# A graph layer's message lists: step columns made by ScalarE, and one product that takes differences

## The chip, the cores and the metric

One core of one Trainium2 chip runs the whole program. The metric is the device time of one execution in microseconds (us), lower is better. The chip has a matrix engine (TensorE, PE), a vector engine (VectorE, DVE), a scalar engine (ScalarE, ACT), a general engine (GpSimd, POOL) and a queue that mostly issues transfers (SyncE, SP). "PEld" is PE's loading of the stationary operand, which overlaps its products.

## The reference

Two layers. The first, a relational graph layer, is the one the change is in; the second is a mixture of experts (16 experts, 2 per token) and takes the second half of the time.

```python
x = x + gnn(layernorm(x), src, dst, edge_type)      # x is [625, 512]
x = x + moe(layernorm(x))

def gnn(input, heads, tails, rel, ...):              # 10625 edges, 8 relations
    h_self = input @ W_self.T + b_self
    H_all = einsum('rod,nd->rno', W_rel, input) + b_rel[:, None, :]   # 16 relations (8 each way)
    msg_to_heads = H_all[rel, tails]
    msg_to_tails = H_all[rel + R, heads]
    agg = segment_sum(msg_to_heads, heads) + segment_sum(msg_to_tails, tails)
    return relu(h_self + agg)
```

## The kernel before

**The products.** H_all has 16 relations by 5 tiles of 125 nodes, so 80 products, numbered i = 0 to 79 (`product`, L819). j = i // 5 is the relation, t = i % 5 the tile. Each is 12 matmuls of 512 columns, since every float32 operand is split into a high and a low part (hi\*hi, hi\*lo, lo\*hi over four chunks). ACT copies each finished product out of PSUM (`take`, L678, its copy is L682), then puts the bias of the product after next into the PSUM buffer that became free (`bias_in`, L691); PE waits for that before product i + 2. SP stores the tile in DRAM (`h_dram`). The weights of relation j + 1 are split while relation j runs: ACT makes the high part of one chunk (`w_main`, L676), DVE the low part (`w_rest`, L503), one chunk in each iteration with t of 1 to 4.

**The lists.** A message is a row of H_all added to a node. The kernel sorts messages into blocks of 128 lanes that belong to one node tile: 90 blocks for direction d = 0, 100 for d = 1. From each edge the number of its block (`block_at`) and its lane in it (`lane`) have been computed in a [125 x 85] layout (`places`, L512). The list, that is which edge stands in which lane of which block, is built by matmul: for each of the 85 edge columns c, DVE writes a one-hot matrix `lane_hot` [125 edges x 128 lanes] (L529) and a matrix `told_hot` [125 edges x blocks, twice] which holds the edge's node and relation at its block (L531 for d = 0, L536 twice for d = 1). PE multiplies the two and adds up over the 85 columns in the PSUM bank `p_list` (`list_chunk`, L848, L855), five columns at a time. Three sets of five columns rotate. `read_list` (L541) then turns `p_list` into the row numbers of the gathers (`row_of`) and the target node of each lane (`seg_of`).

**The messages.** For each block POOL issues an indirect gather of 128 rows from `h_dram` (L400), up to ten blocks ahead. ACT makes their high part (L697), DVE a one-hot matrix of the targets (L555) and the low part (L559), and PE adds both into `p_sum` (L864, L865).

**The order of work is written out by hand.** One loop over i stands in each engine's program, and everything is put into it by tables:

- `columns(d, i)` (L287) says how many of the 85 columns are made before iteration i: `min(85, int(each * (i - begin)))`, with (begin, each) of (4, 5.5) for d = 0 and (24, 3) for d = 1. It gives 5 or 6 columns in each of iterations 4 to 18 and the last three (82 to 84) in iteration 19; for d = 1 it gives 3 in each of iterations 24 to 51 and the last one (84) in iteration 52.
- `chunks(d, i)` (L296): PE multiplies a chunk of five behind product i if its columns were made before iteration i. The last chunk is an exception: it stands behind product 19 for d = 0 and behind product 52 for d = 1, so in the iteration that makes its last columns.
- `due(i)` (L283): three messages per iteration, which PE takes in i = 23 to 37 and from 43 on. ACT and DVE prepare them one iteration earlier.
- `read_list(0)` stands in DVE's iteration 20, behind `told_of(1)`; `read_list(1)` in its iteration 53. `places(1)` stands in DVE's iteration 21, behind that iteration's `w_rest`.

The engines' orders inside an iteration are:

```text
ACT:  w_main, take(i), bias_in(i + 2), [carry_in in i = 8..12], messages
DVE:  w_rest, [told_of(1) in 20, places(1) in 21], columns, read_list, messages
PE:   product(i), list chunks, messages
POOL: waits for rows_ready and the stores, then gathers
```

The function `product` waits for `h_biased`, `message` on PE for `part_lo`, and the first gather for `rows_ready`, which the last instruction of `read_list` (L549) raises. After the 80th product the remaining messages, the self product, a second layernorm and the experts follow in order.

Of the kernel before, what the change touches and what calls it, by code (L numbers as in the profile page):

```python
# [22 lines left out]
P = 128  # L23
# [44 lines left out]
def build(nc, x, edges, w_self, b_self, w_rel, b_rel, router_w, gate_w, up_w, down_w, out):  # L68
    ctx = ExitStack()
    with ctx:  # L70
# [62 lines left out]
        bias_rows_loaded = [sem(f"bias_rows_loaded{i}") for i in range(BIAS_ROWS)]  # L133
        h_stored = [sem(f"h_stored{i}") for i in range(OUTS)]
        list_hot, list_taken, rows_ready = sem("list_hot"), sem("list_taken"), sem("rows_ready")
        part_hi, part_lo, block_done = sem("part_hi"), sem("part_lo"), sem("block_done")
        var2_ready, root2_ready, ln2_ready = sem("var2_ready"), sem("root2_ready"), sem("ln2_ready")
        scale2_ready, xn_hi_ready = sem("scale2_ready"), sem("xn_hi_ready")
# [1 line left out]
        gathers_issued = sem("gathers_issued")  # L140
        x2_full, x2_copied, logits_full = sem("x2_full"), sem("x2_copied"), sem("logits_full")
        round_sems = range(steps.num, logits_full.num + 1)
        assert len(round_sems) == 54 + OUTS + BIAS_ROWS


        ln2_stored, gap_ready, exp_ready = sem("ln2_stored"), sem("gap_ready"), sem("exp_ready")
# [28 lines left out]
        with ExitStack() as g:  # L175
# [5 lines left out]
            x2_whole = sb("x2_whole", [P, T, D], F32, g)  # L181
            x2 = x2_whole[0:TP]
            bias_rows = [x2_whole[:, k] for k in range(BIAS_ROWS)]

            carry = sb("carry", [TP, T, D], F32, g)
            trip = sb("trip", [P, 1], F32, g)
# [100 lines left out]
            def columns(d, i):  # L287

                begin, each = LISTS[d]
                return max(0, min(EC, int(each * (i - begin))))  # L290

            def chunked(d, i):

                return columns(d, i if columns(d, i) == EC else i - 1) // HOT
# [67 lines left out]
            def on_gpsimd(pool, nth_round):  # L362
                q = nc.gpsimd
                done = 0

                def then(instruction):
                    nonlocal done
                    done += 1
                    instruction.then_inc(pool_steps, 1)
                    pool.wait_ge(pool_steps, done)  # L370

                for n, (d, low, _, c) in enumerate(SPANS):
                    if low == 0:
                        q.memset(held[:, d], float(c * P))
                        i = q.memset(first_block[:, d], 0.0)
                i.then_inc(edge_consts, 1)
                q.memset(zero_rows, 0.0).then_inc(route_consts, 1)
                for n, (_, _, _, c) in enumerate(SPANS):
                    q.memset(per_block[:, 0, n * T:(n + 1) * T], 1 / (c * P))
                    i = q.memset(per_block[:, 1, n * T:(n + 1) * T], (c * P + 1) / 2 / (c * P))  # L380
                i.then_inc(edge_consts, 1)
                q.tensor_copy(block_iota[:], iota_i[0:EP, 1:1 + max(IN_DIR)])
                q.tensor_copy(seg_iota[:], iota_i[:, 1:1 + TP])
                q.tensor_copy(slot_iota[:], iota_i[0:TP, 0:P]).then_inc(edge_consts, 1)
                q.iota(token_id_i[:], [[TP, T]], base=1, channel_multiplier=1)
                then(q.iota(spare_row_i[:], [[0, 1]], base=N + 1, channel_multiplier=1))
                q.tensor_copy(token_id[:], token_id_i[:])
                q.tensor_copy(spare_row[:], spare_row_i[:])
                q.tensor_copy(expert_iota[:], iota_i[0:TP, 0:NX])
                q.tensor_copy(tile_iota[:], iota_i[0:1, 0:LISTED])  # L390
                pool.wait_ge(spare_cleared, 64)
                for b in range(BLOCKS):
                    if b in span_at:
                        n = span_at[b]
                        pool.wait_ge(rows_ready, SPANS[n][0] + 1)
                        for k in range(OUTS):
                            pool.wait_ge(h_stored[k], 32 * len(range(k, made(n), OUTS)))
                    if b >= ROWS:
                        pool.wait_ge(part_lo if b - ROWS < last_span else block_done, b - ROWS + 1)
                    q.indirect_dma_start(rows_sb[:, b % ROWS], None, h_dram[0:1 + made(n) * TP],  # L400
                                         bass.IndirectOffsetOnAxis(ap=row_of[:, b:b + 1].bitcast(U32), axis=0)
                                         ).then_inc(gathered[b % ROWS], 16)
                q.tensor_scalar(trip[:], trip[:], 1.0, None, ALU.add).then_inc(gathers_issued, 1)
                pool.wait_ge(gathers_issued, 1)
                pool.wait_ge(round_counted, 1)
                pool.reg_load(rounds_of(pool), n_rounds[0:1, 0:1])

            def on_vector(dve, nth_round):
# [103 lines left out]
                def places(d):  # L512

                    place, here, nth = place_in[:, d], temp[:, 0, d], temp[:, 1, d]
                    then(v.scalar_tensor_tensor(place, place, BIG, held_before[:, d], ALU.subtract, ALU.subtract))
                    v.tensor_tensor(here, place, held[:, d], ALU.is_lt)
                    then(v.tensor_scalar(nth, place, (P - 1) / 2, 1 / P, ALU.subtract, ALU.mult))
                    then(v.tensor_scalar(nth, nth, ROUND, None, ALU.add))
                    v.tensor_scalar(nth, nth, ROUND, None, ALU.subtract)
                    then(v.scalar_tensor_tensor(here, place, 0.0, here, ALU.is_ge, ALU.mult))  # L520
                    v.scalar_tensor_tensor(lane[:, d], nth, -float(P), place, ALU.mult, ALU.add)
                    then(v.scalar_tensor_tensor(nth, nth, 1.0, first_block[:, d], ALU.add, ALU.add))
                    then(v.tensor_tensor(block_at[:, d], nth, here, ALU.mult))

                def column(d, c):
                    n, k, wide = (EC // HOT) * d + c // HOT, c % HOT, IN_DIR[d]
                    if k == 0 and n >= HOT_SETS:
                        dve.wait_ge(list_taken, n - HOT_SETS + 1)
                    v.tensor_scalar(lane_hot[:, n % HOT_SETS, k], slot_iota[:], lane[:, d, c:c + 1], None, ALU.is_equal)  # L529
                    if d == 0:  # L530
                        i = v.scalar_tensor_tensor(told_hot[:, n % HOT_SETS, k, 0:2 * wide].rearrange("p (a b) -> p a b", a=2),  # L531
                                                   block_iota[:, 0:wide].unsqueeze(1).to_broadcast([EP, 2, wide]), block_at[:, d, c:c + 1],
                                                   told0[:, :, c:c + 1].to_broadcast([EP, 2, wide]), ALU.is_equal, ALU.mult)
                    else:
                        for what in range(2):
                            i = v.tensor_scalar(told_hot[:, n % HOT_SETS, k, what * wide:(what + 1) * wide], block_iota[:, 0:wide],  # L536
                                                block_at[:, d, c:c + 1], told1[:, what, c:c + 1], ALU.is_equal, ALU.mult)
                    if k == HOT - 1:
                        i.then_inc(list_hot, 1)

                def read_list(d):  # L541
                    wide, at = IN_DIR[d], IN_DIR[0] * d
                    node, rel_seg, rel = p_list[:, 0:wide], p_list[:, wide:2 * wide], rel_of[:, 0:wide]
                    dve.wait_ge(list_taken, (EC // HOT) * (d + 1))
                    then(v.tensor_scalar(rel, rel_seg, (P - 1) / 2, 1 / P, ALU.subtract, ALU.mult))
                    then(v.tensor_scalar(rel, rel, ROUND, None, ALU.add))
                    then(v.tensor_scalar(rel, rel, ROUND, None, ALU.subtract))
# [67 lines left out]
                for i in range(PRODUCTS):  # L615
# [17 lines left out]
                    for d in range(2):  # L633
                        for c in range(columns(d, i), columns(d, i + 1)):
                            column(d, c)
                        if columns(d, i - 1) < EC and columns(d, i) == EC:
                            read_list(d)
                            if d == 0:
                                round_count()
# [18 lines left out]
            def on_scalar(act, nth_round):  # L658
# [27 lines left out]
                def bias_in(i):  # L686
# [2 lines left out]
                        act.wait_ge(bias_rows_loaded[j % BIAS_ROWS], 16 * (j // BIAS_ROWS + 1))  # L689
                    act.wait_ge(h_taken, i - 1)  # L690
                    s.copy(p_h[0:TP, i % 2], bias_rows[j % BIAS_ROWS][0:TP]).then_inc(h_biased, 1)  # L691

                def message(b):
                    act.wait_ge(gathered[b % ROWS], nth_round * (16 * BLOCKS // ROWS) + 16 * (b // ROWS + 1))
# [55 lines left out]
                for i in range(2, PRODUCTS):  # L750
# [5 lines left out]
                    take(i)  # L756
                    if 8 <= i < 8 + T:
                        carry_in(i - 8)
                    for b in range(due(i), due(i + 1)):
                        message(b)  # L760
                act.wait_ge(gate_loaded, 32)
# [22 lines left out]
            def on_tensor(pe, nth_round):  # L784
# [63 lines left out]
                def list_chunk(d, n):  # L848
                    nth, wide = (EC // HOT) * d + n, 2 * IN_DIR[d]
                    pe.wait_ge(list_hot, nth + 1)  # L850
                    if d and n == 0:
                        pe.wait_ge(rows_ready, d)
                    for k in range(HOT):
                        c = n * HOT + k
                        i = m.matmul(p_list[:, 0:wide], lane_hot[:, nth % HOT_SETS, k], told_hot[:, nth % HOT_SETS, k, 0:wide],  # L855
                                     start=(c == 0), stop=(c == EC - 1))
                    i.then_inc(list_taken, 1)

                def message(b):
                    o = p_sum[0:TP, tile_of[b]]  # L860
# [48 lines left out]
                for i in range(PRODUCTS):  # L909
# [12 lines left out]
                    for d in range(2):  # L922
                        for n in chunks(d, i):
                            list_chunk(d, n)
                    for b in range(due(i - 1), due(i)):
                        message(b)
                left = range(due(PRODUCTS - 1), last_span)
# [810 lines left out]
```

## Time and profile before

| | |
|---|---|
| median of 3 runs | 737.27 us (736.48 to 740.19) |
| the profiled execution | 733.35 us, of which the span of instructions is 731.6 us |
| PE busy | 694.9 us (95%) |
| DVE busy | 625.8 us (86%) |
| ACT busy | 502.0 us (69%) |
| POOL busy | 309.9 us (42%) |
| mean granted TensorE clock | 0.985 of full speed |

Times inside the trace count from the start of the span. A busy time is the union of an engine's instruction spans. What ended an idle time is inferred from semaphore events. The 80 products run from 15 to 348 us, the experts from about 400 us to the end.

### The profile page before, as it was taken

Reading aid. Unit: us, or ns where it says so; the run is one execution under the profiler, and the core shown is the slowest. Engines: PE = TensorE matmul, PEld = TensorE weight load, DVE = VectorE, ACT = ScalarE, POOL = GpSimd, SP = SyncE. Lnnn points to the kernel's source line nnn. Section 1 sums busy time; section 2 is a strip of 40 time slices with the busy share of each in tenths; the row PEclk is TensorE's granted clock in tenths of the full one; section 3 lists DMA queues with packets and bytes.
Section 4 is the critical chain, followed back from the end, with each engine's and each line's share of the span. In section 5 each row is a group of like instructions: output and inputs, shape, how many; then the busy total and the mean of one; then the engine's idle time right before and its main releaser. Section 6 shows DMA issues by size and latency. Waiting matters only on the chain. (4 is left out here: it accounts for less than half of the span.)

```text
span 731.6 us, 10688 instructions
## 1 busy us (share of the span) xinstructions
PE 694.9 (95%) x3210; PEld 542.9 (74%) x3210; DVE 625.8 (86%) x1289; ACT 502.0 (69%) x717; POOL 309.9 (42%) x279
## 2 busy tenths in 40 slices
PE   5899999999998999999997999999999999999993
PEld 4777766777676777777755788888888888888883
DVE  8889979998999677777775899999998999999990
ACT  3655476665675777777556498888877888888870
POOL 3000077851787677777771033332234333333201
PEclk9999999999999999999998899999999999999997
DMA  7347589884888889998767989999999999999932
GB/s 243 126 144 270 168 267 305 299 257 144 301 281 295 276 280 306 315 295 244 217 196 239 379 321 354 405 394 392 405 355 396 370 379 374 361 403 379 357 110 30
DMA packets 54436, 212.75 MB, mean 291 GB/s; under 512 B 9753, under 2 KB 10150, under 8 KB 39158
## 3 DMA queue, kind: packets, MB, share of 16 engines
q1 hardware_dynamic: 34998, 153.85, 55.9%
q0 software_dynamic: 19392, 58.35, 27.4%
q8 instruction: 21, 0.34, 0.2%
q14 instruction: 25, 0.20, 0.1%
HBM read 184.36 MB, written 27.80 MB: 290 GB/s over the span
## 5 line engine op out<-in xcount | busy, mean ns | idle before, releaser
L400 POOL DMA_INDIRECT rows_sb<-h_dram,row_of x190 | 212.5, 1119 | 165.3 <-DVE row_of L549 84.1
L559 DVE TENSOR_TENSOR rows_lo<-rows_sb,rows_hi 128x512 fp32r<-128x512 f32 x175 | 120.1, 686 | 43.5 <-ACT rows_hi L697 43.4
L830 PE MATMUL p_h<-g_hi_sb,xt_hi_whole 128*125 128x512 f32 x320 | 128.4, 401 | 0.3 <-DVE g_lo_sb L503 0.3
L831 PE MATMUL p_h<-g_lo_sb,xt_hi_whole 128*125 128x512 f32 x320 | 126.7, 396 | 0.0
L832 PE MATMUL p_h<-g_hi_sb,xt_lo_whole 128*125 128x512 f32 x320 | 126.5, 395 | 0.0
L697 ACT CAST rows_hi<-rows_sb 128x512 fp32r<-128x512 f32 x175 | 100.1, 619 | 25.5 <-DMA rows_sb<-h_dram,row_of 23.3
L682 ACT COPY h_whole<-p_h 125x512 f32<-125x512 f32 x80 | 46.9, 586 | 89.2 <-PE p_h L832 89.1
L1195 POOL DMA_INDIRECT tokens<-token_dram,rows_of_tokens x15 | 22.1, 1470 | 170.8 <-ACT rows_of_tokens L1484 131.5
L864 PE MATMUL p_sum<-rows_hi,seg_hot 128*125 128x512 f32 x175 | 73.6, 421 | 5.4 <-DVE rows_lo L559 4.5
L1248 DVE TENSOR_TENSOR u_lo_sb<-stage_up,u_hi_sb 128x2048 fp32r<-128x2048 f32 x34 | 76.4, 2288 | 1.0
L1248 DVE TENSOR_TENSOR d_lo_sb<-stage_down,d_hi_sb 128x2048 fp32r<-128x2048 f32 x32 | 71.8, 2286 | 3.0 <-ACT d_hi_sb L1469 2.9
L1599 PE MATMUL p_gate<-g_hi_sb,xt_lo_whole 128*128 128x512 f32 x256 | 74.1, 401 | 0.0
L1248 DVE TENSOR_TENSOR g_lo_sb<-stage_gate,g_hi_sb 128x2048 fp32r<-128x2048 f32 x32 | 71.9, 2287 | 1.1 <-ACT g_hi_sb L1469 1.1
L1599 PE MATMUL p_up<-u_hi_sb,xt_lo_whole 128*128 128x512 f32 x256 | 72.7, 395 | 0.0
L832 PEld LDWEIGHTS p_h<-g_hi_sb,xt_lo_whole 128*125 128x125 f32 x320 | 59.6, 186 | 15.1
L830 PEld LDWEIGHTS p_h<-g_hi_sb,xt_hi_whole 128*125 128x125 f32 x320 | 59.8, 187 | 14.6 <-issue 0.3
L831 PEld LDWEIGHTS p_h<-g_lo_sb,xt_hi_whole 128*125 128x125 f32 x320 | 59.8, 187 | 14.1
L865 PE MATMUL p_sum<-rows_lo,seg_hot 128*125 128x512 f32 x175 | 69.1, 395 | 0.0
L1469 ACT CAST u_hi_sb<-stage_up 128x2048 fp32r<-128x2048 f32 x34 | 63.3, 1914 | 4.1 <-PEq L1011 4.1
L1469 ACT CAST g_hi_sb<-stage_gate 128x2048 fp32r<-128x2048 f32 x32 | 59.6, 1915 | 6.5 <-PE p_gate L1599 6.5
L1469 ACT CAST d_hi_sb<-stage_down 128x2048 fp32r<-128x2048 f32 x32 | 59.6, 1916 | 0.0
L1206 POOL DMA_INDIRECT out<-y_sb,rows_of_out x16 | 30.4, 1899 | 66.5 <-ACT y_sb L1509 66.2
(292 smaller groups left out, 1363.6 us busy)
## 6 DMA issues: line engine op xcount, KB each, us to landing
stage_up<-in_L_ffn_up_w SPq DMA_DIRECT2D x34, 1024.0 KB, 8.0
stage_gate<-in_L_ffn_gate_w SPq DMA_DIRECT2D x32, 1024.0 KB, 8.7
stage_down<-in_L_ffn_down_w SPq DMA_DIRECT2D x32, 1024.0 KB, 7.5
h_dram<-h_whole SPq DMA_DIRECT2D x80, 224.0 KB
stage_up<-in_L_gnn_W_rel SPq DMA_DIRECT2D x16, 1024.0 KB, 8.0
x_whole<-in_L_gnn_b_rel SPq DMA_DIRECT2D x16, 256.0 KB, 9.7
rows_sb<-h_dram,row_of POOLq DMA_INDIRECT x190, 5.1
h_dram<-h_whole SPq DMA_DIRECT2D x80, 26.0 KB
```

The lines of the kernel that those rows point to most:

```text
L400: q.indirect_dma_start(rows_sb[:, b % ROWS], None, h_dram[0:1 + made(n) * TP], bass.IndirectOffsetOnAxis(ap=row_of[:, b:b + 1].bitcast(U32 ...
L559: v.tensor_tensor(rows_lo[:, b % PARTS], rows_sb[:, b % ROWS], rows_hi[:, b % PARTS].bitcast(F32), ALU.subtract).then_inc(part_lo, 1)
L682: s.copy(h_sb[:, i % OUTS], p_h[0:TP, i % 2]).then_inc(h_taken, 1)
L697: s.copy(rows_hi[:, b % PARTS], rows_sb[:, b % ROWS]).then_inc(part_hi, 1)
L830: m.matmul(o, xt_hi[:, dc, at], wt_hi_sb[:, 1 - j % 2, dc], start=(by_matmul and dc == 0), stop=False, skip_group_check=True)
L831: m.matmul(o, xt_hi[:, dc, at], wt_lo_sb[:, 1 - j % 2, dc], start=False, stop=False, skip_group_check=True)
L832: last = m.matmul(o, xt_lo[:, dc, at], wt_hi_sb[:, 1 - j % 2, dc], start=False, stop=False, skip_group_check=True)
L864: m.matmul(o, seg_hot[:, b % HOTS], rows_hi[:, b % PARTS], start=False, stop=False, skip_group_check=True)
L865: m.matmul(o, seg_hot[:, b % HOTS], rows_lo[:, b % PARTS], start=False, stop=False, skip_group_check=True).then_inc(block_done, 1)
L1248: v.tensor_tensor(half(w_lo[k][:], k, i), staged(k, e, i), half(w_hi[k][:], k, i).bitcast(F32), ALU.subtract).then_inc(split_lo[k], 1)
L1469: s.copy(half(w_hi[k][:], k, i), staged(k, e, i)).then_inc(split_hi[k], 1)
L1599: i = m.matmul(into[:, h * 512:(h + 1) * 512], x_part[of_first(e)][:, c], w_part[k][:, c, h * 512:(h + 1) * 512], start=(c == 0 and x_part ...
```

## The change

The lane matrix is no longer a one-hot matrix. ACT writes, for each column, the sign of (m + 0.5 - lane) over the lanes m = 0 to 127: -1 below the edge's lane and +1 from it on. PE adds these up as before, so that `p_list` holds running sums over the lanes. DVE halves them into SBUF (`halve`), and one float32 product with a [128 x 128] matrix of differences (`difference`) writes the list into `p_list`. DVE no longer makes lane columns. POOL makes the constants at the start. `list_end(d)` is the first iteration in which all columns have been made: 20 and 53.

```diff
+            differ, shifted, corner = [x2_whole[:, 3, k * P:(k + 1) * P] for k in range(3)]
+            between = x2_whole[0:TP, 3, 3 * P:4 * P].bitcast(F16)[:, 0:P]
+            sums = x2_whole[:, 4, 0:2 * max(IN_DIR)]
...
+            def list_end(d):
+                return min(i for i in range(PRODUCTS) if columns(d, i) == EC)
...  on POOL, behind tile_iota and ahead of the wait for spare_cleared
+                q.tensor_scalar(between, iota_i[0:TP, 0:P], 0.5, None, ALU.add).then_inc(steps_made, 1)
+                q.affine_select(out=shifted, in_=ones[:], compare_op=ALU.is_equal, fill=0.0, base=1, pattern=[[-1, P]], channel_multiplier=1)
+                then(q.affine_select(out=corner, in_=ones[:], compare_op=ALU.is_equal, fill=0.0, base=1 - P, pattern=[[-1, P]],
+                                     channel_multiplier=1))
+                then(q.tensor_tensor(differ, ident[:], shifted, ALU.subtract))
+                q.tensor_tensor(differ, differ, corner, ALU.add).then_inc(steps_made, 1)
...  on DVE, in places(d), column(d, c), and read_list(d)
-                    v.scalar_tensor_tensor(lane[:, d], nth, -float(P), place, ALU.mult, ALU.add)
+                    v.scalar_tensor_tensor(lane[:, d], nth, float(P), place, ALU.mult, ALU.subtract).then_inc(placed, 1)
...
-                    v.tensor_scalar(lane_hot[:, n % HOT_SETS, k], slot_iota[:], lane[:, d, c:c + 1], None, ALU.is_equal)
...
+                def halve(d):
+                    dve.wait_ge(list_taken, (EC // HOT) * (d + 1))
+                    if d:
+                        dve.wait_ge(differed, d)
+                    v.tensor_scalar(sums[:, 0:2 * IN_DIR[d]], p_list[:, 0:2 * IN_DIR[d]], 0.5, None, ALU.mult).then_inc(halved, 1)
...
-                    dve.wait_ge(list_taken, (EC // HOT) * (d + 1))
+                    dve.wait_ge(differed, d + 1)
...  DVE's loop
-                        if columns(d, i - 1) < EC and columns(d, i) == EC:
+                        if i == list_end(d):
+                            halve(d)
+                        if i == list_end(d) + 1:
                             read_list(d)
                             if d == 0:
                                 round_count()
...  on ACT
+                def lane_step(d, c):
+                    n, k = (EC // HOT) * d + c // HOT, c % HOT
+                    if c == 0:
+                        act.wait_ge(placed, d + 1)
+                        if d == 0:
+                            act.wait_ge(steps_made, 1)
+                    if k == 0 and n >= HOT_SETS:
+                        act.wait_ge(list_taken, n - HOT_SETS + 1)
+                    i = s.activation(lane_hot[:, n % HOT_SETS, k], between, ACT.Sign, bias=lane[:, d, c:c + 1], scale=1.0)
+                    if k == HOT - 1:
+                        i.then_inc(lane_steps, 1)
...  ACT's loop, behind take(i) and carry_in, ahead of the messages
+                    for d in range(2):
+                        for c in range(columns(d, i), columns(d, i + 1)):
+                            lane_step(d, c)
...  on PE
                     pe.wait_ge(list_hot, nth + 1)
+                    pe.wait_ge(lane_steps, nth + 1)
...
+                def difference(d):
+                    if d == 0:
+                        pe.wait_ge(steps_made, 2)
+                    pe.wait_ge(halved, d + 1)
+                    m.matmul(p_list[:, 0:2 * IN_DIR[d]], differ, sums[:, 0:2 * IN_DIR[d]], start=True, stop=True).then_inc(differed, 1)
...  PE's loop, behind the chunks and ahead of the messages
+                        if i == list_end(d):
+                            difference(d)
```

## Rows read from the trace of the kernel before

**Rows 1.** Busy time by stretch: us, then PE, PEld, DVE, ACT, POOL; clock; DMA
```profile
118.00:165.00 47.00, 46.77 (x211) 34.16 (x210) 47.00 (x161) 32.80 (x60) 33.06 (x27) 1.00 0.85 278
190.00:228.00 38.00, 37.85 (x171) 27.85 (x172) 38.00 (x130) 26.78 (x49) 30.38 (x26) 1.00 0.87 287
```

**Rows 2.** Timeline (start, us): ACT takes products 18, 19, 21, 22, 30, 35
```profile
83.96 0.59 ACT L682 COPY h_whole<-p_h 125x512 f32<-125x512 f32 x1 [1.47 <-PE p_h L832]
...
87.17 0.59 ACT L682 COPY h_whole<-p_h 125x512 f32<-125x512 f32 x1 [1.39 <-PE p_h L832]
...
94.18 0.59 ACT L682 COPY h_whole<-p_h 125x512 f32<-125x512 f32 x1 [1.01 <-PE p_h L832]
...
96.97 0.59 ACT L682 COPY h_whole<-p_h 125x512 f32<-125x512 f32 x1 [1.03 <-PE p_h L832]
...
135.29 0.59 ACT L682 COPY h_whole<-p_h 125x512 f32<-125x512 f32 x1 [1.96 <-PE p_h L832]
...
158.59 0.59 ACT L682 COPY h_whole<-p_h 125x512 f32<-125x512 f32 x1 [1.96 <-PE p_h L832]
```

**Rows 3.** Timeline: a column of the second list on DVE
```profile
132.21 0.25 DVE L529 TENSOR_SCALAR lane_whole<-slot_iota,lane 125x128 f16<-125x128 f16 x1
...
132.37 0.75 DVE L536 TENSOR_SCALAR told_whole<-block_iota,block_at,told 125x100 f16<-125x100 f16 x2
```

**Rows 4.** Groups of instructions by form, ACT: busy us, mean ns, idle before
```profile
L676 ACT CAST g_hi_sb<-stage_up 128x512 fp32r<-128x512 f32 x64 | 38.9, 618 | 0.0
...
L674 ACT ACTIVATE g_hi_sb<-stage_up,first 128x512 fp32r<-128x512 f32 x4 | 2.9, 722 | 0.0
...
L725 ACT ACT_TABLE_LOAD x1 | 1.3, 1283 | 4.7 <-PEq L949 4.7
```

**Rows 5.** Timeline: three copies of 512 columns in a row on ACT
```profile
103.52 1.67 ACT L697 CAST rows_hi<-rows_sb 128x512 fp32r<-128x512 f32 x3
```

**Rows 6.** ACT's idle time ahead of the takes: 43 to 70 us
```profile
  PE p_h L832: 10.7, 8
```

**Rows 7.** Timeline: the take of product 13, PE's chunks behind product 14
```profile
67.48 0.59 ACT L682 COPY h_whole<-p_h 125x512 f32<-125x512 f32 x1 [0.92 <-PE p_h L832]
...
70.48 0.95 PE L855 MATMUL p_list<-told_whole,lane_whole 125*128 125x180 f16 x10
```

**Rows 8.** ACT's idle time ahead of the takes: 76 to 89 us
```profile
  PE p_h L832: 5.8, 4
```

**Rows 9.** Timeline: PE's last chunk of the first list
```profile
88.00 0.56 PE L855 MATMUL p_list<-told_whole,lane_whole 125*128 125x180 f16 x5 [0.46 <-DVE told_whole L531]
```

**Rows 10.** Timeline: reading the first list, the first gather, the first messages
```profile
90.45 0.25 DVE L545 TENSOR_SCALAR rel_of<-p_list 128x90 f32<-128x90 f32 x1
...
91.38 0.24 DVE L549 SCALAR_TENSOR_TENSOR row_of<-rel_of,p_list 128x90 int32<-128x90 f32 x1
...
92.52 1.19 POOL L400 DMA_INDIRECT rows_sb<-h_dram,row_of  x1 [84.14 <-DVE row_of L549]
...
93.20 0.70 DVE L503 TENSOR_TENSOR g_lo_sb<-stage_up,g_hi_sb 128x512 fp32r<-128x512 f32 x1 [0.36 <-ACT g_hi_sb L676]
...
95.59 0.25 DVE L523 TENSOR_TENSOR block_at<-temp 125x85 f32<-125x85 f32 x1
...
102.68 0.51 PE L864 MATMUL p_sum<-rows_hi,seg_hot 128*125 128x512 f32 x1 [1.64 <-DVE rows_lo L559]
```

**Rows 11.** Timeline: seven float32 matmuls of 512 columns in a row
```profile
378.92 3.17 PE L871 MATMUL p_sum<-rows_sb,told_whole 128*125 128x512 f32 x7
```

**Rows 12.** Timeline: the take of product 52, the second list's last chunk
```profile
231.00 0.59 ACT L682 COPY h_whole<-p_h 125x512 f32<-125x512 f32 x1 [0.80 <-PE p_h L832]
...
233.20 0.60 PE L855 MATMUL p_list<-told_whole,lane_whole 125*128 125x200 f16 x5 [2.24 <-DVE told_whole L536]
```

**Rows 13.** Timeline: two later waits of PE for messages, products 26 and 43
```profile
117.41 0.49 PE L864 MATMUL p_sum<-rows_hi,seg_hot 128*125 128x512 f32 x1 [1.23 <-DVE rows_lo L559]
...
189.91 0.49 PE L864 MATMUL p_sum<-rows_hi,seg_hot 128*125 128x512 f32 x1 [0.89 <-DVE rows_lo L559]
```

More of the change, by code:

```diff
@@ L135, in build @@
         list_hot, list_taken, rows_ready = sem("list_hot"), sem("list_taken"), sem("rows_ready")
+        steps_made, placed, lane_steps, halved, differed = sem("steps_made"), sem("placed"), sem("lane_steps"), sem("halved"), sem("differed")
         part_hi, part_lo, block_done = sem("part_hi"), sem("part_lo"), sem("block_done")
@@ L142, in build @@
         round_sems = range(steps.num, logits_full.num + 1)
-        assert len(round_sems) == 54 + OUTS + BIAS_ROWS
+        assert len(round_sems) == 59 + OUTS + BIAS_ROWS
         ln2_stored, gap_ready, exp_ready = sem("ln2_stored"), sem("gap_ready"), sem("exp_ready")
```

## Prediction

> **What bounds the kernel now.** I read the busy time by stretch first. While the second list is made and messages flow, PE is busy nearly throughout, but DVE is busy for the whole of both stretches, ACT for 70% [rows 1]. Two engines can't both be the bound, so I asked the timeline how long a product lasts. ACT takes each product when it ends, so the takes are a clock. A product alone lasts 2.79 us (96.97 - 94.18), thus a matmul 0.2325; with one chunk of the first list it is 3.21 (87.17 - 83.96), so a chunk costs 0.42; with three messages, six matmuls more, it should be 4.18. From product 30 to 35 there are three chunks: 5 x 4.18 + 3 x 0.42 = 22.2. Measured is 23.3 [rows 2]. So DVE does set the pace there, by 0.22 us a product, in small waits that a busy share hides. In the first list DVE does not: PE's steps there are those of its own work.
>
> The messages start tightly: PE waits for the third one, at 102.68, and this goes back to the first gathers, which POOL issued at 92.52 as soon as the list was read [rows 10]. What the change does to that moment matters as much as what it takes from DVE.
>
> **The change part by part.**
>
> *DVE loses the lane columns.* One has a span of 0.25, but the next instruction starts 0.16 behind it [rows 3]: 0.16 is what it costs in a row. Three per iteration give 0.48, more than the 0.22 by which DVE holds PE back. So PE becomes the bound. Some 20 products (27 to 37, 44 to 52) were paced by DVE: 20 x 0.22 = -4.4 us. Of the large wait ahead of the second list's last chunk (2.24, [rows 12]) a part goes: ACT makes column 84 behind the take of product 52 at 231.00, so at 231.00 + 0.62 + 0.53 + 0.40 + 0.05 = 232.6 instead of 233.2: -0.6.
>
> *The price of a step on ACT.* No row shows a Sign over 128 columns. A copy of 512 columns takes 0.62 and one that reads a scale from SBUF 0.72, so a pointer costs 0.10 [rows 4]. Three copies in a row take 1.67, so each overlaps the next by 0.10 [rows 5]. With some 0.82 ns a column (estimated: an instruction of 512 columns less a fixed part near 0.2), 128 columns take 0.62 - 0.32 + 0.10 = 0.40 alone and 0.30 in a row. Bounds are 0.20 (the pointer free) and 0.40 (no overlap). I take 0.30. The Trainium skill (ScalarE: Activation LUTs, What ACT_TABLE_LOAD costs) gives 280 ns + 0.833 N with a pointer bias and 93 ns of overlap, 0.294 in a row; by it the sum below would be 0.4 less. The same page (Rules for kernel authors) tells authors to do plain arithmetic on VectorE rather than on ScalarE. It speaks against this move, and the rows agree: 0.16 there, 0.30 here.
>
> *First list, ACT falls behind: +2.2.* Ahead of the takes of products 6 to 13 ACT idled 10.7 us in all [rows 6]; iterations 5 to 12 get 44 steps, 13.2 us. So the take of product 13 comes 2.5 late, at 69.95. Its six steps end at 69.95 + 1.15 (two copies, take and bias: 0.62 + 0.53) + 6 x 0.30 + 0.1 = 73.0. PE wants all of them for the second chunk behind product 14, which it began near 70.85 [rows 7]: +2.15. With steps of 0.24 or less it is nothing (44 x 0.24 is 10.7); with 0.40 it is about 6.
>
> *The last chunk of the first list: +2.1.* From there to product 19 ACT gets 22 steps more, 6.6 us against 5.8 idle [rows 8], and is 0.8 late again. Columns 82 to 84 are made behind take 19, since ACT's order ties them to it, while DVE made them while PE was still in product 19. So 87.17 + 0.8 + 1.15 + 0.9 + 0.1 = 90.1, against 88.0 [rows 9].
>
> *The differences: +0.8.* A float32 matmul of 512 columns takes 0.43 in a row [rows 11]. One of 180 or 200 columns with its load I put at 0.4, between 0.2 and 0.6; two of them. DVE halves (0.25) while PE is in the product ahead, so this hides.
>
> *The list is read an iteration later: +5.4.* This is the largest term and no instruction of it is new. Before, `read_list(0)` ran in DVE's iteration 20, from 90.45 to 91.62. Now it stands in iteration 21, and there behind two things. `w_rest` waits for ACT's `w_main`, which stands behind take 20: it ran from 93.20 to 93.90. Then `places(1)` ran to 95.84 [rows 10]. So `read_list` can end at 95.84 + 1.2 = 97.0 on the old clock, 5.4 later. The first gather moves from 92.52 to 97.9. Message 2 was already waited for, so what was late by 0 is now late by 5.4, and PE stands for it. POOL issues the later ones at its own pace, so they don't catch up. Bounds: 4 (landings are quicker away from the weight transfers) and 6. The second list's delay costs nothing: its gathers also need product 54 in DRAM, stored after take 54, and that ends later than DVE's `read_list(1)`.
>
> *POOL's five constants* run at the start, where POOL then waits 84 us for the list [rows 10]: nothing, or some tenths if they disturb DVE. ACT's steps among the messages (0.9 per iteration) fit its idle time in rows 1 (30% of a product, 1.4 us). If that cover is gone, messages come late: a rival below.
>
> **Sum:** 2.2 + 2.1 + 0.8 + 5.4 - 4.4 - 0.6 = +5.5 us. The experts start that much later, nothing there changes. The profiled execution took 733.35, the median of the runs is 737.27; on the median: 742.8. A measurement of this kernel can tell about 0.5% (3.7 us) from no change; the forecast is +0.75%.
>
> **The rivals.**
>
> 1. *ACT hides its steps and the messages make it up; not slower.* At 0.24 a step or less, the first list costs 0, its last chunk 1.1, the differences 0.8, the late reading 5.4. Against it 4.4 + 0.6, and PE's later waits for messages (1.23 and 0.89, [rows 13]) end too, as a DVE with time in hand prepares them earlier: +0.2, so 737.5. It decides at 0.24 us a step. For it: ACT idled before every take. Against: 0.30 from rows 4 and 5, and the wait at 117.41 looks like one for a gather, which a late start doesn't help. Chance 0.22. If the gathers landed faster too, it would reach faster by over 0.5%; I leave that 0.07 on top.
>
> 2. *The gathers or ACT bound the message stretch.* With steps of 0.3, ACT's iteration is 1.15 + 0.9 + 1.67 + 0.53 = 4.25 against PE's 4.18 to 4.6, and a late start leaves less lead for gathers. Then the 4.4 doesn't come: +9.9, 747.2. For it: little margin. Against: the sum per product still stays below PE's with a chunk. Chance 0.12.
>
> 3. *Sign needs tables of its own.* A table load takes 1.28 [rows 4]; one ahead of the first step would find ACT idle or add to its lag, a second ahead of the square roots after the messages would lie on the path: +6.8 to +8, about 744. Chance 0.05. The Trainium skill (ScalarE: Activation LUTs, Table sets) says that cheap functions such as relu, copy, identity and abs stand in every set; it doesn't name Sign there, and no run here shows it.
>
> **How the numbers follow.** My forecast has 0.54, and 0.44 of that is above +3.7. Slower: 0.44 + 0.12 + 0.05 = 0.61, less a hundredth for the measurement. Same: 0.10 of the forecast and rival 1's 0.22, 0.32. Faster: 0.07 and that hundredth, 0.08. The range takes in rival 1 at its lower end and rival 2 at its upper: 737 to 748.
>
> **What would show it.** Right: the lane rows on ACT start 0.30 apart in a row; ACT has no idle time ahead of takes 9 to 13; PE waits about 2 us for an ACT lane row behind product 14 and again behind product 19; L549's instruction ends more than 5 us later against the end of product 20, and PE's first message waits 4 to 6 us for `rows_lo`; five products in the message stretch take 22.2 rather than 23.3; no ACT_TABLE_LOAD more. Wrong: steps of 0.24 or less with no waits behind product 14; a first gather that is not late against product 20; message iterations still at 4.78, or gathers named as what ends ACT's waits in them.

## The result, and the profile after

The changed kernel takes 740.22 us (median of 20 runs, 737.31 to 747.01), the kernel before 737.95 (20 runs beside them). The ratio is 1.0044, 95% interval 1.0024 to 1.0065: slower by 3.2 us, 1.8 to 4.8. The medians alone differ by 2.3. The forecast was 742.8 with a range of 737 to 748. Its +5.5 us has the right sign but lies above that interval. Two executions, one of e1 below (746.71) and one of the kernel before beside e9 to e11 (745.35), lay over 1.5% above their fastest and are left out of the ratios.

The profiled executions differ by more: 740.55 against 733.35. The profiled execution of the kernel before was faster than each of its 20 timed runs (the lowest is 734.91). So the trace tells where time goes, and the ratios how much.

Busy time of each engine in the page after (us, share of the span, instructions):

```profile
PE 697.9 (94%) x3214; PEld 547.2 (74%) x3214; DVE 601.1 (81%) x1121; ACT 549.4 (74%) x887; POOL 309.9 (42%) x284
```

DVE lost 25 us of work and ACT gained 47; PE has 3 us more. The waits of PE (who waited for whom, total us, times, longest):

```profile
PE p_sum L909 <- DVE rows_lo L579: 7.7, 8, 3.0
PE p_list L893 <- ACT lane_whole L723: 4.7, 3, 2.1
```

In the first, the longest had been 1.64 [rows 10]; the second is new: two of its three stand where PE had waited for DVE, 0.46 and 2.24 [rows 9, 12], one behind product 14. The stretch of the first list and the first messages, in order of time (start, us, what, the idle time before it):

```profile
71.76 0.47 PE L893 MATMUL p_list<-told_whole,lane_whole 125*128 125x180 f16 x4 [0.89 <-ACT lane_whole L723]
...
88.26 0.57 ACT L704 COPY h_whole<-p_h 125x512 f32<-125x512 f32 x1
...
90.52 0.55 PE L893 MATMUL p_list<-told_whole,lane_whole 125*128 125x180 f16 x5 [2.12 <-ACT lane_whole L723]
...
97.26 0.69 DVE L518 TENSOR_TENSOR g_lo_sb<-stage_up,g_hi_sb 128x512 fp32r<-128x512 f32 x1 [4.39 <-ACT g_hi_sb L698]
...
99.62 0.25 DVE L538 TENSOR_TENSOR block_at<-temp 125x85 f32<-125x85 f32 x1
...
100.83 0.24 DVE L569 SCALAR_TENSOR_TENSOR row_of<-rel_of,p_list 128x90 int32<-128x90 f32 x1
...
107.11 0.50 PE L909 MATMUL p_sum<-rows_hi,seg_hot 128*125 128x512 f32 x1 [3.02 <-DVE rows_lo L579]
108.71 0.79 PE L909 MATMUL p_sum<-rows_hi,seg_hot 128*125 128x512 f32 x1 [0.87 <-DVE rows_lo L579]
```

These answer to [rows 7, 9, 10]. DVE stands idle for 4.39 us for ACT's `w_main`, then splits the weight, places the second list, and only then reads the first, as forecast: the list is complete near 95.6 and read at 101.1. The first gather goes out at 101.97, 6.5 us after the take of product 20 (95.47); before it was 1.1 us after it (92.52 and 91.41). That is the 5.4 of the forecast to the tenth. What it cost is another matter (below).

The steps: three in a row take 0.98 us, one alone 0.40, so the next starts 0.29 behind. ACT has no idle time at all ahead of the takes of products 6 to 13, where it had 10.7 us [rows 6].

```profile
116.91 0.98 ACT L723 ACTIVATE lane_whole<-x_whole,lane 125x128 f16<-125x128 f16 x3
...
144.22 0.59 ACT L704 COPY h_whole<-p_h 125x512 f32<-125x512 f32 x1 [0.97 <-PE p_h L869]
...
166.62 0.59 ACT L704 COPY h_whole<-p_h 125x512 f32<-125x512 f32 x1 [1.01 <-PE p_h L869]
```

The last two rows are the takes of products 30 and 35: 22.4 us for the five, where [rows 2] had 23.3. PE now sets the pace there, and ACT still idles about 1 us ahead of a take.

Something that no term of the forecast had: the granted TensorE clock. Busy time by stretch (us, then PE, PEld, DVE, ACT, POOL; the third figure from the end is the granted clock), and PE's matmuls inside the second stretch:

```profile
91.00:95.00 4.00, 4.00 (x12) 3.12 (x12) 1.74 (x10) 0.00 (x0) 0.00 (x0) 0.57 0.85 304
108.00:115.00 7.00, 6.29 (x14) 4.53 (x15) 5.99 (x15) 4.43 (x8) 5.48 (x6) 0.51 0.74 220
115.00:122.00 7.00, 7.00 (x30) 5.34 (x30) 4.44 (x16) 5.68 (x14) 5.48 (x6) 1.00 0.84 250
```

```profile
111.31 0.63 PE L868 MATMUL p_h<-g_lo_sb,xt_hi_whole 128*125 128x512 f32 x1
111.74 0.63 PE L869 MATMUL p_h<-g_hi_sb,xt_lo_whole 128*125 128x512 f32 x1
```

Behind PE's wait of 2.12 us, and again behind those of 3.02 and 0.87, the clock is at 1.2 GHz, and matmuls start 0.43 apart instead of 0.23. In the profiled execution of the kernel before, the clock was full throughout this stretch, with waits of at most 1.64 there. But it was full, too, behind the same wait of 2.12 in the profiles of e1 and e7 below. This is e1's row for the first of these stretches:

```profile
91.00:95.00 4.00, 4.00 (x20) 3.26 (x20) 2.42 (x14) 1.06 (x2) 0.00 (x0) 1.00 0.81 293
```

In e5, e9 and e12 it was low there again. So this half clock is not a fixed part of the change: it comes in some executions of that wait and not in others.

### The profile page after: what moved, and what is told of

Read it like the earlier page. It is cut to its first block and busy times, and to the rows that moved or that the text cites. A ratio compares the mean times of both kernels' runs of the same rounds, so it can differ in the third digit from the quotient of the medians.

```text
span 738.8 us, 10740 instructions
## 1 busy us (share of the span) xinstructions
PE 697.9 (94%) x3214; PEld 547.2 (74%) x3214; DVE 601.1 (81%) x1121; ACT 549.4 (74%) x887; POOL 309.9 (42%) x284
## 5 line engine op out<-in xcount | busy, mean ns | idle before, releaser
L867 PE MATMUL p_h<-g_hi_sb,xt_hi_whole 128*125 128x512 f32 x320 | 130.1, 406 | 1.1 <-ACT p_h L713 0.8
L868 PE MATMUL p_h<-g_lo_sb,xt_hi_whole 128*125 128x512 f32 x320 | 128.3, 401 | 0.0
L518 DVE TENSOR_TENSOR g_lo_sb<-stage_up,g_hi_sb 128x512 fp32r<-128x512 f32 x64 | 43.4, 686 | 28.8 <-ACT g_hi_sb L698 28.8
```

The source lines that it names most:

```text
L867: m.matmul(o, xt_hi[:, dc, at], wt_hi_sb[:, 1 - j % 2, dc], start=(by_matmul and dc == 0), stop=False, skip_group_check=True)
L868: m.matmul(o, xt_hi[:, dc, at], wt_lo_sb[:, 1 - j % 2, dc], start=False, stop=False, skip_group_check=True)
```

## The experiments

Theory: three independent terms, late reading of the first list (slower), ACT's load in the first list (slower), relief of DVE in the second (faster). Rivals: ACT's load explains all of the loss; the clock is a term of its own; the gathers set the time whatever is mended. Each kernel below was timed against the kernel before in the same series; a ratio of 1.001 is 0.74 us. Where two rows are compared, their difference is known to 2.5 to 4 us either way. Differences in us below are from the ratios.

| kernel | median us | ratio to before, 95% |
|---|---|---|
| the changed kernel | 740.22 | 1.0044 (1.0024 to 1.0065) |
| e1 changed, list read in iteration 20 | 736.58 | 0.9992 (0.9965 to 1.0019) |
| e2 before, list read in iteration 21 | 741.25 | 1.0050 (1.0025 to 1.0074) |
| e3 changed, last steps ahead of the take | 740.88 | 1.0054 (1.0022 to 1.0087) |
| e4 only the second list by steps | 731.79 | 0.9927 (0.9895 to 0.9958) |
| e5 changed, matmuls that bridge the wait | 743.25 | 1.0073 (1.0043 to 1.0103) |
| e6 e1 and e3 together | 737.35 | 1.0003 (0.9976 to 1.0031) |
| e7 only the first list by steps | 743.66 | 1.0096 (1.0056 to 1.0135) |
| e8 e4, last column made first | 731.82 | 0.9935 (0.9904 to 0.9966) |
| e9 changed, messages begun two products later | 735.77 | 0.9975 (0.9945 to 1.0005) |
| e11 before, messages begun two products later | 731.14 | 0.9921 (0.9889 to 0.9953) |
| e10 e8, messages begun two products later | 728.44 | 0.9878 (0.9836 to 0.9920) |
| e12 e1, messages begun two products later | 732.06 | 0.9907 (0.9872 to 0.9943) |

**e1, the list read in iteration 20**

```diff
-                        if i == list_end(d) + 1:
+                        if i == list_end(d) + d:
                             read_list(d)
```

> The changed kernel with the first list read in DVE's iteration 20 again, right behind its halving, ahead of that iteration's successor's w_rest and places. Theory 'late reading' (the move of read_list by one iteration is the largest cost): the first gather comes some 4.6 us earlier against product 20 than in the changed kernel, PE's wait for the first messages (3.0 + 0.9 us) shrinks to under 2, and with it the half clock behind it; total 4 to 7 us less than the changed kernel, so 0 to 3 us less than the kernel before. Rival 'ScalarE's load' (ACT's steps cost it all): the first gather moves but the messages stay late because ACT is; less than 1.5 us gained on the changed kernel.

Measured: 0.9992, so 3.8 us less than the changed kernel's 1.0044. The first gather goes out at 96.28 instead of 101.97, and PE's one wait for the first messages is 1.35 us (102.68 had 1.64 in [rows 10]). A little under the expected 4 to 7 and above the rival's 1.5, though with 2.5 us either way it doesn't exclude the rival by itself. A later wait for messages is longer, 1.80 at 120.01 against 1.23 in [rows 13].

**e2, the late reading alone, in the kernel before**

```diff
-                        if columns(d, i - 1) < EC and columns(d, i) == EC:
+                        k = i if d else i - 1
+                        if columns(d, k - 1) < EC and columns(d, k) == EC:
                             read_list(d)
```

> The kernel before with nothing changed but that the first list is read in DVE's iteration 21, behind w_rest and places, as in the changed kernel. Late reading: slower than before by 4 to 7 us (5.4 of waiting for the first messages, with or without some half clock behind it), that is about 742 to 745. ScalarE's load: within 1.5 us of before.

Measured: 1.0050, +3.7 us (1.8 to 5.5), a little under the expected 4 to 7, with no step on ACT at all. Its timeline, first gather and first messages:

```profile
96.54 0.24 DVE L549 SCALAR_TENSOR_TENSOR row_of<-rel_of,p_list 128x90 int32<-128x90 f32 x1
97.67 1.19 POOL L400 DMA_INDIRECT rows_sb<-h_dram,row_of  x1 [89.28 <-DMA h_dram<-h_whole]
...
101.22 0.62 ACT L698 CAST rows_hi<-rows_sb 128x512 fp32r<-128x512 f32 x1 [3.28 <-DMA rows_sb<-h_dram,row_of]
...
102.62 0.49 PE L865 MATMUL p_sum<-rows_hi,seg_hot 128*125 128x512 f32 x1 [3.15 <-DVE rows_lo L559]
...
104.09 0.79 PE L865 MATMUL p_sum<-rows_hi,seg_hot 128*125 128x512 f32 x1 [0.74 <-DVE rows_lo L559]
```

The first gather is where the forecast had put it (97.9). But ACT has its rows 3.55 us after the issue. The third gather, the one that PE had waited for, landed 6.0 us after its issue before and 3.6 here. So PE's first message is 3.1 us later than before (102.62 and 99.54), and its third 2.8, not 5.4. Behind the wait the clock falls, and product 24 is taken at 111.44, 5.2 later than before. Two products on, PE waits 0.35 where it waited 1.23 [rows 13], and the lateness is 4.1 and stays so (product 42 is taken at 188.89, before at 184.88). Moving one call by an iteration is about half of the whole loss; ACT's load is out as its only cause.

**e4, only the second list by steps.** The first list's lane columns stay on DVE, without halving and difference, read in iteration 20.

```diff
+                    if d == 0:
+                        v.tensor_scalar(lane_hot[:, n % HOT_SETS, k], slot_iota[:], lane[:, d, c:c + 1], None, ALU.is_equal)
...
-                    for d in range(2):
+                    for d in range(1, 2):
                         for c in range(columns(d, i), columns(d, i + 1)):
                             lane_step(d, c)
```

> Only the second list's lane columns are made by ACT as steps and differenced; the first list is made and read as before. My sum for this part alone: products 27 to 37 and 44 to 51 at the pace of PE, -0.12 to -0.22 us each (-2.4 to -4.4), -0.6 ahead of the last chunk, +0.4 for one difference: 2.5 to 4.5 us less than before. Rival 'gathers or ACT bound the message stretch': no gain, within 1 us of before or slower.

Measured: 0.9927, 5.4 us less (3.1 to 7.7), more than the expected 2.5 to 4.5, and faster than both kernels. So ACT and the gathers don't take the gain away. Gathers still cost something: its profiled execution is one of its two slowest (735.24, the median is 731.79), and in it PE waits 0.99 at 140.94 for messages. The same windows as [rows 1]:

```profile
118.00:165.00 47.00, 45.95 (x215) 35.35 (x213) 43.15 (x131) 41.06 (x91) 30.64 (x28) 1.00 0.88 292
190.00:228.00 38.00, 37.94 (x178) 29.46 (x177) 35.99 (x110) 34.28 (x75) 29.46 (x29) 1.00 0.91 300
```

In the same time PE does 215 and 178 matmuls instead of 211 and 171, DVE is no longer full, ACT has gone from 33 to 41 us of 47.

**e7, only the first list by steps**, the other half, read in iteration 21 as in the change (the mirror image of e4's edit).

> The other half of the change: only the first list by ACT's steps and a difference, read in DVE's iteration 21; the second list made and read as before. If the change is the sum of its halves, this half costs what the second-list half gained plus what the whole costs: 5.4 + 3 = some 8 us more than before (745 to 747). My own sum for it: about 1.1 behind product 14, 2.1 to 2.5 ahead of the last chunk, 0.4, and 3.7 to 5.4 of late reading: 7.3 to 9.4. Rival 'the halves share a cost' (clock or gathers): under 6.

Measured: 1.0096, +7.1 us (4.1 to 10), just under the 7.3 to 9.4 of my own sum. The halves add up to +1.7, the whole is +3.2; their intervals take that in. Of the 7.1, late reading is 3.7 (e2), so ACT's load in the first list is some 3.4; from e1 less e4 it is 4.8.

**e3, ACT's last steps ahead of the take**

```diff
+                    for d in range(2):
+                        if i == list_end(d) - 1:
+                            for c in range(columns(d, i), columns(d, i + 1)):
+                                lane_step(d, c)
                     take(i)
...
-                        for c in range(columns(d, i), columns(d, i + 1)):
-                            lane_step(d, c)
+                        if i != list_end(d) - 1:
+                            for c in range(columns(d, i), columns(d, i + 1)):
+                                lane_step(d, c)
```

> The changed kernel with ACT's last steps of each list (columns 82 to 84, and 84) ahead of the takes of products 19 and 52 instead of behind them. Tie to the take: PE's waits of 2.1 and 1.7 us ahead of the last chunks fall, the first to under 0.7, the second to what DVE's told column leaves (1.7 before in the second-list kernel, so 0 to 0.3 saved); the half clock behind product 19 goes with the first (1.5 us): 2 to 4 us less than the changed kernel. Rival: the first gathers depend on w_main and the takes, not on the chunk, and the saving is eaten by the wait for the first messages: under 1 us.

Measured: 1.0054, nothing gained that 2.8 us either way could show. The wait only changes its name and keeps 1.69 of its 2.12:

```profile
90.09 0.56 PE L898 MATMUL p_list<-told_whole,lane_whole 125*128 125x180 f16 x5 [1.69 <-DVE told_whole L545]
```

DVE's columns 82 to 84 stand behind its `w_rest`, and that behind ACT's `w_main`, which is late because of the steps before it. The take was not the only tie. In its profile product 20 is taken 2.0 us earlier, but 1.6 of that is the half clock, which is gone in e1 too, where the wait is unchanged. Against e1's 93.91 the edit gives 0.4 (93.51). The waits for the first messages (2.97, 0.81, 0.82) take 0.7 of the lead back. The rest doesn't vanish there: it is 2.3 us at product 42 and 1.4 at product 79, but the two profiled executions end alike (740.71 and 740.55), so this is within what executions differ by.

**e6, e1 and e3 together**

> Both mends at once: first list read in iteration 20, last steps ahead of the takes. If the terms add: 2 to 4 us less than the kernel with only the reading mended (736.6), that is 733 to 735, at the level of the second-list kernel or up to 2 us above (lag behind product 14 and one difference remain). Rival: gathers behind the weight transfer at product 25 set the time, and everything earlier is given back there: 736 to 737.

Measured: 1.0003 against 0.9992 for e1: nothing gained again; 737.35 is above both ranges, nearest the rival's. Its profile has product 20 at 93.53, 0.4 ahead of e1, as in e3: that is all that moving ACT's steps gives.

**e8, in e4 the last column made first on both engines**, ahead of the take and of `w_rest`.

> The second-list kernel (731.8) with its last column (84) made ahead of the take of product 52 on ACT and ahead of w_rest on DVE. PE's wait of 1.7 us ahead of the last chunk falls below 0.3: 1 to 1.6 us less, 730 to 731. If a later wait (gathers near product 61) takes it up: no difference.

Measured: 0.9935 against 0.9927, no difference, where 1 to 1.6 us less was expected. In the profile product 53 is taken 5.8 us after product 52 instead of 6.5, so 0.7 of the 1.7 went, too little to tell.

**e5, 16 matmuls of 512 columns behind product 23**, their result not used. They are extra work in PE's order and keep it at work while the first gathers land.

```diff
+                    if i == 23:
+                        pe.wait_ge(rows_ready, 1)
+                        for _ in range(16):
+                            m.matmul(p_list[0:TP, :], xt_hi[:, 0, 0:TP], xt_lo_whole[:, 0:512], start=True, stop=True)
```

> The changed kernel with 16 extra matmuls of 512 columns on PE behind product 23 (their result is not used), ahead of the wait for the first messages. They take 3.7 us at full clock inside a wait of over 3.9 us. Theory 'clock' (the halving behind that wait costs time of its own): TensorE stays at full clock behind the wait, product 24 lasts 2.8 us instead of 4.7, total 1.5 to 3 us less than the changed kernel. If the half clock is hidden by the gathers that are late anyway: within 1 us of the changed kernel.

Measured: 1.0073, 2.1 us more than the changed kernel, known to 2.7 either way. So the expected 1.5 to 3 us less is excluded, and whether it is really slower is not shown. The clock did stay full behind this wait: product 24 came 3.89 us after product 23, where the changed kernel needed 6.25. But PE then waited for the next gathers:

```profile
123.72 0.50 PE L909 MATMUL p_sum<-rows_hi,seg_hot 128*125 128x512 f32 x1 [1.06 <-DVE rows_lo L579]
126.30 0.50 PE L909 MATMUL p_sum<-rows_hi,seg_hot 128*125 128x512 f32 x1 [1.85 <-DVE rows_lo L579]
```

At product 25 it is 2.1 us ahead of the changed kernel, at product 27 it is 1.8 behind, and the clock falls behind these waits instead (0.50 near 129 to 131 us). So keeping the clock up behind the first messages bought nothing, since the next gathers were late as well. It isn't shown that a half clock there costs nothing of its own, because it only came three products later. Why the kernel was 1.8 us behind the changed one by then stays open.

**e9, e11, e10, e12: the messages begun two products later**

```diff
-LAG, START, PACE = 3, 22, 3.0
+LAG, START, PACE = 3, 24, 3.0
```

> The changed kernel with the messages begun two products later on every engine (START 24 instead of 22): PE does products 24 and 25 while the first gathers land. If late reading costs only because PE stands waiting for the first messages: no waits of 3.0 and 0.9 us, no half clock behind them, and the three to six messages moved fit between products 38 and 42, where PE takes none now. 3.5 to 6 us less than the changed kernel (734 to 737). If gathers behind the weight transfer near product 25 set the time: under 1.5 us less.

> The control: the kernel before with START 24. Its waits there are smaller (1.64 and 1.23 us at 102.68 and 117.41): 1 to 3 us less than before (734.5 to 736.5). So the changed kernel should gain more by this edit than the kernel before does, by about the 3.7 us that late reading costs; if both gain the same, late reading has another cost than PE's waiting.

> The kernel with only the second list by ACT's steps, its last column made first, and START 24. 731.8 less the 1 to 3 us of the control: 729 to 731, faster than both kernels. If the gain of the second list and the later start are the same time counted twice (PE's waits for messages): 731 to 732.

> The changed kernel (both lists by ACT's steps) with the list read in iteration 20 and START 24: late reading and the waits for the first messages are both gone, ACT's load in the first list stays. Against the control (kernel before with START 24, 731.1): second list -3 to -5.4, first list (wait behind product 14, wait of 2.1 ahead of its last chunk, half clock behind it, two differences) +4 to +5: 730 to 733, so 2 to 4 us above the kernel with only the second list by ACT (728.4). Rival: the first list's load cost only through the messages it made late; then 727 to 729.

Measured: the changed kernel gains 5.1 us (0.9975), as expected. But the control gains 5.8 (0.9921), twice what I gave it, no less than the changed kernel, and so the second half of its expectation is refuted: late reading is not just PE's standing at the first messages. The profiles show why. In e11 no wait for a message is left between products 20 and 60; in e9 the first gather is still at 101.95 against 92.29, and the wait moves on:

```profile
110.34 0.50 PE L909 MATMUL p_sum<-rows_hi,seg_hot 128*125 128x512 f32 x1 [0.66 <-DVE rows_lo L579]
...
118.52 0.50 PE L909 MATMUL p_sum<-rows_hi,seg_hot 128*125 128x512 f32 x1 [1.11 <-DVE rows_lo L579]
```

e12 against e9 is the reading alone under the later start: 0.9907 against 0.9975, 5 us (3.4 either way; 2.4 at product 42 of the profiles). e10, with only the second list by steps, is the best kernel of this study: 728.44 us, 0.9878, 9.0 us less than before and 3.2 less than e11 (3.9 either way, so that e10 is faster than e11 is not shown). e12 stands 2.1 us above e10 by the ratios (3.6 by the medians): inside what was expected, though the intervals of the ratios overlap. In the profiles the first list by steps costs 4.4 us at product 42 (184.24 against 179.80), 1.6 of it half clock, where PE's waits for the first messages are the same 0.66 in both.

## Why the prediction was right, and which terms were not

The forecast was +5.5 us, slower, by three terms up and one down. The direction and the chain hold, and late reading and the second list are the large terms, as said. In the profiles each of the four large terms came out smaller than forecast, those up and the one down, so part of the errors cancels, and that the total fell inside the range is in part luck. Point by point:

- **DVE was the bound in the message stretch, and PE is now.** Right: five products take 22.4 (forecast 22.2). The size is less sure. The forecast gave 0.22 to each of 20 products. In the profiles, from the take of product 26 to that of 37 it is 50.93 us before and 49.06 after, and from 43 to 52 it is 41.45 before and, where no wait for a gather falls in, 40.3 (e9, e12): 1.9 and 1.1, together 3.0 for the 4.4. In the changed kernel's own profile the second stretch took 41.44, with a wait for messages of 0.81 in it, and gained nothing. The last chunk gave its 0.6 (product 53 is taken 6.50 after product 52, before 7.05). With one difference that is -3.2, and e10 less e11 gives 3.2 less too. e4 measured -5.4 (3.1 to 7.7), where the forecast's terms gave -4.6; the interval takes in both.
- **The price of a step.** Right: 0.29 in a row for 0.30. Here the Trainium skill's figure (ScalarE: Activation LUTs, What ACT_TABLE_LOAD costs), 0.294, was nearer than my estimate from copies. Its advice to do plain arithmetic on VectorE (Rules for kernel authors) fits the first list (e7 lost 7.1 us) and not the second (e4 gained 5.4): what decided was which engine had time left.
- **First list, ACT falls behind: +2.2.** Mis-sized: it was 1.1 (product 15 is taken 34.84 us after product 5, before 33.72). ACT's idle time was used up to the last, as said, but the take of product 13 is only 1.3 us late (28.25 after that of product 5, before 26.92) and not 2.5, and PE's wait is 0.89 at 71.76. I had counted 10.7 of idle time from the ends of ACT's instructions. Once they stand in a row they overlap: the take of product 13 begins 0.51 behind the start of `w_main` (68.57 and 68.06), which alone takes 0.62. Over eight iterations that is an estimated 0.9 of further room: 44 x 0.29 - 10.7 - 0.9 = 1.2.
- **The last chunk: +2.1.** Mis-sized too: 1.7. 88.00 became 90.52, and since this execution was 0.24 ahead at product 5, that is 2.8 later, of which 1.1 was there before. ACT was not 0.8 late again; from product 13 to 19 the takes are 19.69 us apart in both kernels. The reason was half of it: e3 shows that DVE's column, tied to `w_main`, keeps 1.69 of the wait when ACT's steps are out of the way. For both terms together the forecast had 4.3. In this profile product 20 is taken 4.3 late, but 1.6 of that is the half clock: a coincidence.
- **The differences: +0.8.** The take of product 21 follows that of product 20 after 3.10 us instead of 2.77, so one difference costs 0.33; both 0.7.
- **Late reading: +5.4.** The step that was mis-sized most. The gather is late by 5.4 to the tenth, but it costs 3.7 (e2), 3.8 (changed less e1). I had written that later gathers do not catch up. POOL indeed issues them no faster, but they land sooner: the third took 3.6 us in e2 and 6.0 before. The lower bound of 4 had allowed for quicker landings; they belonged in the term. A later wait (1.23 at 117.41) was also shorter by 0.9 in e2. The runs put the cost at the lower bound or under it, which their interval of 1.8 to 5.5 doesn't settle.
- **What the sum left out:** the clock behind the waits. In the profile it lengthens product 20 by 1.6 us (taken 7.21 us after product 19, in e1 5.65 with the same wait). Behind the first messages e5 didn't find a gain in keeping it up.

By the ratios: 3.7 (late reading) plus 3.4 to 4.8 (first list; the forecast had 2.2, 2.1 and a difference, 4.7) minus 5.4 (second list) is 1.7 to 3.1; measured 3.2. Each of these is known to 2 or 3 us either way, so the runs show the signs and the rough sizes. Rival 1 is out as it was put: a step takes 0.29, and PE waits for ACT's steps three times. But my argument against it, that a late start doesn't help a wait for a gather, fails in e2, where the wait of 1.23 became 0.35 with DVE's load as it was. Rival 2 is refuted by e4, and rival 3 by the profile, which has three table loads as before (the first again 1283 ns, the next only at 412 us).

What stays open: what makes the gathers near products 25 and 26 slow. A transfer of the next relation's weights is issued there. In the kernel before it ran from 107.64 to about 115 us, and the five gathers issued from 107.7 to 113.5 took 7.8 us (median), where those from 92 to 105 took 4.9 and those from 116 to 121 took 4.8. In the changed kernel the slow ones come at 116 to 123, with the transfer. They go together in every profile here, but no run took the transfer away.

## What to carry to other kernels

When a hand-written order moves a step to the next iteration, cost everything that stands ahead of it there and what those things wait for: moving `read_list` behind `w_rest` and `places` cost 3.7 us, about as much as the list's 85 extra instructions on another engine. Move work to an idle engine only in the stretch in which the old engine is the bound: the second half of this change alone gained 5.4 us, the first half alone lost 7.1. And where a consumer waits at the start of a stream, first try beginning it later: one constant gave 5.8 us here.

## What the runs showed of the hardware that I had not expected

The granted TensorE clock fell from 2.4 to 1.2 GHz behind some of PE's waits, and the length of the wait alone didn't decide it. In the changed kernel's profile it was low for 3.5 us behind the wait of 2.12 and for 6.9 behind those of 3.02 and 0.87. Behind the same wait of 2.12 it was low in e5, e9 and e12, and full in e1 and e7. In the kernel before no low stretch followed the waits of 1.64 and 1.23, in e3 none the 1.69. But in e1 one followed a wait of 1.80 at 120.01, and in e8 one of 1.38 at 118.11 (with 1.05 just before it, at 116.00). The 20 timed runs of the changed kernel go with a cost of this kind: the five above 745 have a mean clock of 0.976 to 0.981, the seven under 739 one of 0.979 to 0.985. A new wait of 2 us can thus cost up to 1.6 more in one execution and nothing in the next.

The time from the issue of a gather to its rows was not one number: 3.5 to 9.2 us in the kernel before, with a median of 5.1. Those issued during a weight transfer took about 8, and the third gather, issued 5 us later in e2, took 3.6 where it had taken 6.0. So a start that is late by 5.4 us doesn't have to cost 5.4.
